# Context key/value projections as three fp16 products of split operands in place of one float32 product

## What is computed

```
# layer 0, cross-attention (context rows are layer-normed first)
k, v = split(ctx @ wkv);  q = _rope(q); k = _rope(k)
# layer 2, cross-attention
k = ctx @ Wk;  v = ctx @ Wv
# layers 1 and 3, cross-attention (W_ctx and W_k are folded to one 96 x 128 weight)
ctx = text_embed @ W_ctx + b_ctx;  k = ctx @ W_k;  v = ctx @ W_v
```

## Time and profile before

| | |
|---|---|
| time, median of 3 runs | 6562.08 us (6561.17 to 6566.58) |
| the profiled execution: its own time from first to last instruction (the span; the page gives no other) | 6568.9 us |
| TensorE busy | 6072.1 us, 92% of the span |
| VectorE busy | 4851.4 us, 74% |
| ScalarE busy | 4175.0 us, 64% |
| GpSimd busy | 2747.1 us, 42% |
| mean granted TensorE clock | 0.967 of full speed |

### The profile page before, as it was taken

How to read it: one execution, slowest core, us unless ns; L and a number is a source line. 1 busy time by engine, 2 the same in 40 slices (tenths; PEclk the granted TensorE clock), 3 DMA queues, 4 the chain that set the end, 5 groups by cost and what they waited for, 6 DMA issues and landing times.

```text
span 6568.9 us, 122562 instructions
## 1 busy us (share of the span) xinstructions
PE 6072.1 (92%) x42376; PEld 3586.6 (55%) x42376; DVE 4851.4 (74%) x9782; ACT 4175.0 (64%) x9228; POOL 2747.1 (42%) x2358
## 2 busy tenths in 40 slices
PE   7999999989899998998989999899898999989988
PEld 5566456654556645664455654566445665456644
DVE  6887776657788777675878877667578886876656
ACT  4556676656655668665765666766575566776656
POOL 3466115751246612564025651266402655126630
PEclk8999999999999999998999999999898999999989
DMA  3111011100111101111011100111001111011100
GB/s 87 36 33 26 22 35 31 28 25 19 48 34 33 27 21 37 30 32 28 13 50 36 33 27 19 38 30 33 23 18 49 31 30 30 16 41 30 28 20 12
DMA packets 347662, 204.18 MB, mean 31 GB/s; under 512 B 165005, under 2 KB 319981, under 8 KB 346926
## 3 DMA queue, kind: packets, MB, share of 16 engines
q1 hardware_dynamic: 347054, 196.34, 11.8%
HBM read 105.18 MB, written 1.05 MB: 16 GB/s over the span
## 4 chain that ended last, share of the span: by engine, by line
PE 73%; DVE 10%; ACT 7%; issue 5%; POOL 4%; SPq 1%; DVEq 0%; DMA 0%; POOLq 0%; ACTq 0%
PE ring L1347 37%; PE o_acc L1347 18%; PE scores L1347 17%; DVE max_part L2097 3%; POOL weight_sum L1309 3%; ACT probs L1782 2%; ACT qop L1636 2%; DVE o_inv L2120 1%; POOL qm L1328 1%; DVE region L2059 1%; DVE qop L2056 1%; ACT qm L1636 1%; DVE ring L2073 1%; PE ring L1451 0%; DVE ring L2076 0%
## 5 line engine op out<-in xcount | busy, mean ns | idle before, releaser
L2097 DVE TENSOR_REDUCE max_part<-ring 128x1 f32<-128x400 f32 (+2 forms) x4608 | 2412.7, 577 | 567.4 <-PE ring L1347 543.8
L1782 ACT ACTIVATE probs<-scores 128x512 f32<-128x512 f32 (+1 forms) x3840 | 2105.9, 599 | 1051.5 <-PE scores L1347 961.8
L1309 POOL TENSOR_TENSOR weight_sum<-weight_sum,probs 128x512 f32<-128x512 f32 (+1 forms) x1408 | 1785.7, 1268 | 201.9 <-ACT probs L1782 66.8
L1347 PE MATMUL o_acc<-probs,region 128*32 128x256 f32 (+2 forms) x13312 | 1348.2, 388 | 11.3 <-ACT probs L1782 6.8
L1636 ACT ACTIVATE region<-ring 64x400 f16<-64x400 f32 (+4 forms) x1744 | 820.4, 480 | 480.6 <-PE ring L1347 291.9
L1309 POOL TENSOR_TENSOR weight_sum<-probs 128x512 f32<-128x512 f32 x256 | 325.4, 1271 | 1619.5 <-PE ring L1347 1194.3
L1347 PEld LDWEIGHTS o_acc<-probs,region 128*32 128x32 f32 (+2 forms) x13312 | 586.0, 122 | 547.0 <-issue 202.4
L1347 PE MATMUL scores<-qop,region 128*128 128x256 f16 (+1 forms) x3328 | 804.1, 274 | 11.3 <-ACT qop L1636 7.8
L1347 PE MATMUL scores<-qop,x_cop 128*128 128x256 f16 (+1 forms) x3328 | 800.1, 273 | 0.0
L1347 PE MATMUL ring<-nk,qm 128*128 128x400 f16 (+2 forms) x2560 | 709.5, 337 | 51.9 <-DVE max_part L2097 19.7
L1347 PE MATMUL scores<-qm,nk 128*128 128x512 f16 (+1 forms) x1920 | 657.3, 389 | 62.1 <-ACT probs L1782 32.0
(11 more groups left out here) (170 smaller groups left out, 7265.9 us busy)
## 6 DMA issues: line engine op xcount, KB each, us to landing
x_cop<-region SPq DMA_DIRECT2D x256, 200.1 KB, 3.1
stage<-in_wide SPq DMA_DIRECT2D x512, 64.0 KB, 2.0
nk<-region SPq DMA_DIRECT2D x192, 100.1 KB, 2.2
stage<-in_wide SPq DMA_DIRECT2D x128, 128.0 KB, 2.6
v_stage<-in_wide SPq DMA_DIRECT2D x256, 64.0 KB, 1.9
wo_stage<-in_wide SPq DMA_DIRECT2D x32, 512.0 KB, 4.0
cop_few<-kop_few SPq DMA_DIRECT2D x256, 32.0 KB, 1.9
ff_w<-in_ff_w SPq DMA_DIRECT2D x24, 256.0 KB, 3.4
```

The costliest lines, as they stand in the source:

```text
L1309: pool.tensor_tensor(total, before, probs[0:rows_, (un.chunk + k) % PROBS, :], ALU.add)\
L1347: return pe.matmul(out, lhs, rhs, start=start, stop=stop, skip_group_check=True)
L1782: act.activation(to, src, ACT.Exp, scale=t.scale).then_inc(exp_done.sem, 1)
L2097: dve.tensor_reduce(dst, src, AX.X, ALU.max).then_inc(*release(one))
```

## The change

Each operand of a context projection is held as two fp16 numbers, high and low, whose sum is close to the float32 value, and the product is made as high x high + high x low + low x high in one PSUM bank. The wide weights are multiplied by 32 before they are split (`GAIN`); the scale of the exponential and that of the value copy take it out again.

- Weights of 1 and 7: once at the start, 8 groups each are read from the input blob to `region`, ScalarE writes the high half, VectorE the low half (into the space of `ctx_t` and `src_t`), and SyncE stores both to DRAM (`kv_split`). These are the 16 "split" items. A unit then loads its weights from there, in place of the float32 ones.
- Context: ScalarE writes the high half, VectorE the low half, and VectorE gives back the bank. For `src_t` ScalarE first applies scale and bias within the bank.
- The folded narrow weights get the same treatment in `fold_w`.
- The planner gets new costs, new waits and the split items, so that the lists of all engines change.

```diff
+            def in_halves(out, lhs, rhs):
+                mm(out, lhs[0], rhs[0], True, False)
+                mm(out, lhs[0], rhs[1], False, False)
+                return mm(out, lhs[1], rhs[0], False, True)
...
-                        last = mm(out[:, 0:w], stage[0:t.dk, w_at, k, W_K:W_K + P], src[0:t.dk, a0:a0 + w], True, True)
+                        if t.cross:
+                            halves = k_split_of(un)
+                            last = in_halves(out[:, 0:w], [halves[:, k, l, :] for l in range(2)],
+                                             [src[:, l, a0:a0 + w] for l in range(2)])
...
+                                last = in_halves(out[0:r, m * P:(m + 1) * P], [src[:, l, at:at + r] for l in range(2)],
+                                                 [halves[:, l, :] for l in range(2)])
...
+SPLITS = [(s, g) for s in (1, 7) for g in range(H // 2)]
...
+    for i in range(len(SPLITS)):
+        put(2.0 + 6.0 * i, "split", i)
...
+    def split(self, due, one):
+        self.part("ACT", "split", due, one, 0.4, [])
+        self.part("DVE", "split", due, one, 0.55, [("ACT", one)])
+        self.part("SP", "split", due, one, 0.6, [("DVE", one)], 4.0)
...
-            self.part("PE", "op", due, one, 0.1 + w * 0.00155, deps, 0.2)
+            self.part("PE", "op", due, one, 0.06 + w * 0.00128 if t.cross and i else 0.1 + w * 0.00155, deps, 0.2)
...
             load_hidden_weights(0)
+            sp.dma_start(kv_in[1][:, :, 0, :], a["wide1"][:, 0:DC, SK:SV].rearrange("g p c -> p g c")).then_inc(kv_loaded[0], 16)
...
+            wait((mod_full, 1))
+            for k, at in enumerate((SK, SV)):
+                sp.dma_start(kv_in[7][:, :, k, :], a["wide7"][:, 0:DC, at:at + P].rearrange("g p c -> p g c"))\
+                    .then_inc(kv_loaded[1], 16)
             program()
...
+                def split_high_weights(i):
+                    s, g = SPLITS[i]
+                    if g == 0:
+                        act.wait_ge(kv_loaded[s // 7], 48 if s == 1 else 32)
+                    copy(kv_out[s][:, g, :, 0, :], kv_in[s][:, g, :, :], scale=GAIN).then_inc(kv_high, 1)
...
                         if j < 4:
-                            last = copy(ctx_t[:, u % 2, a0:a0 + w], out[0:DC, 0:w])
+                            copy(ctx_t[:, u % 2, 0, a0:a0 + w], out[0:DC, 0:w]).then_inc(ctx_high.sem, 1)
                         else:
-                            last = copy(src_t[0:DC, u % 2, a0:a0 + w], out[0:DC, 0:w], scale=cols[0:DC, C_CLNW:C_CLNW + 1],
-                                        bias=cols[0:DC, C_CLNB:C_CLNB + 1])
+                            copy(out[0:DC, 0:w], out[0:DC, 0:w], scale=cols[0:DC, C_CLNW:C_CLNW + 1],
+                                 bias=cols[0:DC, C_CLNB:C_CLNB + 1]).then_inc(ctx_high.sem, 1)
+                            copy(src_t[:, u % 2, 0, a0:a0 + w], out[0:DC, 0:w]).then_inc(ctx_high.sem, 1)
+                        return
...
+                def context_low(one, j):
...
+                    dve.tensor_tensor(to[:, 1, :], ring[0:DC, bank(one), 0:w], to[:, 0, :], ALU.subtract).then_inc(*release(one))
```

More of the change, by code:

```diff
@@ L45, in __init__ @@
         self.chunks = self.kt * self.halves
-        self.scale = float((64 if wide else 8) ** -0.5)
+        self.gain = GAIN if cross and wide else 1.0
+        self.scale = float((64 if wide else 8) ** -0.5) / self.gain
         self.dk = DC if (cross and wide) else D
@@ L517, in job, with weights @@
         (self.wide_job if t.wide else self.narrow_job)(due, one, un, t, n, j, kind, i, k, pe)
+    def weights(self, un):
+        if un.wide_at + 2 < len(self.wide) and self.wide[un.wide_at + 2].t.cross:
+            return [("SP", ("split", len(SPLITS) - 1))]
+        return []
     def inputs(self, un):
@@ L541, in wide_job @@
             if j == t.last_op:
-                self.part("SP", "load", due, one, 2.1 if t.rope else 1.4, [pe], 2.5)
+                self.part("SP", "load", due, one, 2.1 if t.rope else 1.4, [pe, *self.weights(un)], 2.5)
         elif kind == "low":
@@ L1036, in values_of, with k_split_of, v_split_of @@
             return (x_nv if un.t.cross else nv_few)[:, un.u % 2, :, :]
+        def k_split_of(un):
+            sets = 2 if un.t.rope else 1
+            halves = stage[0:DC, un.wide_at % 2, 0:sets, :].bitcast(F16)
+            return halves[:, :, 2 * W_K:2 * W_K + 2 * P].rearrange("p s (l c) -> p s l c", l=2)
+        def v_split_of(un):
+            return v_stage[0:DC, un.wide_at % 2, :].bitcast(F16).rearrange("p (l c) -> p l c", l=2)
         def split_of(s, u, kind):
@@ L1095, in load_weights @@
                 src = blob[un.p, :, 0:sets * SQS].rearrange("p (s c) -> p s c", s=sets)
+                if un.t.cross and un.u == 0 and un.p == 0:
+                    wait((kv_stored, 16 * len(SPLITS)))
                 for k in range(sets):
@@ L1526, in wide_job @@
                         for m in range(nt):
-                            r = t.rows(t0 + m)
-                            last = mm(out[0:r, m * P:(m + 1) * P], src[0:t.dk, (t0 + m) * P:(t0 + m) * P + r],
-                                      v_stage[0:t.dk, w_at, :], True, True)
+                            r, at = t.rows(t0 + m), (t0 + m) * P
+                            if t.cross:
+                                halves = v_split_of(un)
+                                last = in_halves(out[0:r, m * P:(m + 1) * P], [src[:, l, at:at + r] for l in range(2)],
+                                                 [halves[:, l, :] for l in range(2)])
+                            else:
+                                last = mm(out[0:r, m * P:(m + 1) * P], src[:, at:at + r], v_stage[:, w_at, :], True, True)
                     elif kind == "shift":
@@ L1646, in store_values @@
                         elif m1 > m0:
-                            last = copy(to[0:n, t0 + m0:t0 + m1, :], src[0:n, m0 * P:m1 * P].rearrange("p (m c) -> p m c", c=P))
+                            last = copy(to[0:n, t0 + m0:t0 + m1, :], src[0:n, m0 * P:m1 * P].rearrange("p (m c) -> p m c", c=P),
+                                        scale=1.0 / t.gain)
                     return last
@@ L2027, in pre @@
                         load(u)
+                    elif kind == "ctx":
+                        context_low(one, j)
+                    elif kind == "fold":
+                        fold_low(one)
                     elif kind == "stats":
```

121 lines of the change are left out of this document (93 added, 28 removed).

## The result

The changed kernel takes 6530.08 us (median of 4 runs, 6529.27 to 6534.0), the kernel before 6564.33 (4 runs, 6561.17 to 6570.43): ratio 0.9949, 95% interval 0.9935 to 0.9963. It is faster by half a per cent, 34 us, where 205 were forecast; 6530 lies above the range of 6290 to 6460.

What follows compares the result with a forecast made beforehand. TensorE's own work bounds attentions 1 and 7. Of 274 us raw saving 230 arrive; less 13 for the start and 12 for context halves, 205 off 6562 gives 6357 us (own range 6310 to 6400, wider 6290 to 6460).

Steps and rivals of the forecast that it cites:

- The prices: TensorE's context projections: fp16 matmuls start 0.17 us apart at 400 columns, 0.055 at 128-column value tiles; raw sum 274 us.
- half hidden: Rival: weight loads hide only half, value matmuls 0.082 us apart, total 6484; chance 0.07.
- exposed (0.109) weight loads: Rival: each fresh 128-column fp16 load bounds its value matmul at 0.109 us, total 6616; chance 0.05.
- I take 30 of 39: Attention 1: of 39 us TensorE saves per stage, 30 arrive (ends 15 and 39), 120 us in all.
- the halves of the context: Stages of attention 0: splitting the context adds 3 us for each of four stages, 12 us (ends 0 and 30).
- the clock of 1.00 in attention 1: Attention 1: the granted clock was read as 1.00, full speed (2.4 GHz), in the kernel before.
- The rival in which VectorE takes over: Attention 1: VectorE can't be filled beyond 90%, stage ends at 404 us, 18 saved, total 6405; chance 0.17.
- Attention 7: Attention 7: no other engine is close, so 23 of 24 us per stage arrive, 92 us.
- The narrow part: Narrow attentions' context projections: 18 of 23 us saved arrive.
- The start: Program start: splitting delays the first queries to 52 us and first scores to 64, 13 us lost (ends 6 and 17).
- a load takes SyncE 0.65 us at most: Start: issue time per load on SyncE, taken as 0.5 us, so the last two loads are issued by 45.6.
- no longer late: Start: the late `v_stage` load, about 4 us of waiting before the first scores, no longer costs time.

Runs made afterwards that it cites:

- 9: Changed kernel, attention 1: TensorE's last two attn x V groups of a unit moved right ahead of the next unit's first scores; 6521.17 us, 0.9935.
- 11: Changed kernel with attention 1's last two attn x V groups moved ahead of the next first scores and its maximum over half of the columns; 6472.55 us, 0.9861.
- 7: Changed kernel's operations, but the planner reckons TensorE's context projections with the durations of the kernel before; 6496.74 us, 0.9896.
- 12: Changed kernel, VectorE computes each low half of the normed context twice, the first into a tile nothing reads; 6554.8 us, 0.9988.
- 10: Changed kernel planned with the old projection durations, and VectorE's maximum in attention 1 over half of the columns; 6447.95 us, 0.9822.
- 1: Changed kernel, ScalarE splits attention 7's weights only after TensorE has begun the first unit's values; 6531.64 us, 0.9951.
- 8: Changed kernel, weight splits later on all queues, the three loads for attention 1's splits issued behind the narrow weights; 6512.94 us, 0.992.
- 4: Changed kernel with attention 1 back in float32 (its splits, source halves and three products undone); 6537.21 us, 0.9962.

## Why the prediction was wrong

**The prices: right.** 0.17 and 0.0575 us against 0.17 and 0.055. The rivals of half hidden (0.082) and of exposed (0.109) weight loads are refuted. The Trainium skill's 81 ns a matmul (page "TensorE: Matmul & The Clock Gate", section "Back-to-back issue gap") does not hold for this stream, whose matmuls are 57 ns apart. The low half of a context piece, taken at 700 ns, lasts 684:

```profile
L2024 DVE TENSOR_TENSOR src_t<-ring,src_t 96x512 f16<-96x512 f32 x24 | 16.4, 684 | 12.5 <-ACT src_t L1725 12.5
```

**"I take 30 of 39" in attention 1: the step that failed.** It was 120 us, its low end (15 a stage) still 60; measured 2. Four things are in it.
- It weighed VectorE by its mean over the stage, 359 of 422 or 85%. That mean holds the entries and ends, where VectorE waits. In the units that repeat it was already 92.5 of 103.7, 89%, so with VectorE's work as it is the unit got from 25.9 to 24.8 at best in the orders tried (9), half of the saving; with half of the maxima it reached 24.2 (11).
- It took the order of the lists as given. The planner gets the new durations, and its new list moved ready work out of the one place where TensorE must wait for VectorE and ScalarE in turn. The new order as a whole cost 31 us in attention 1 (7), this gap about 13 of them (9). Both lists could be read beforehand, and this gap stands in the new one.
- It gave a price to the halves of the context only in the stages of attention 0, 12 us, where half of them do lie. The other half it put into VectorE's mean in attention 1 (364 of 383). If computing them once costs what computing them again did (12), those in attention 0 cost 7 and those in attention 1, which had no price, 16.
- It took the clock of 1.00 in attention 1 as given; at most 15 us went there.

These overlap and do not add up to the 118 us that are missing: the order (31) and the halves (16) make 47; halving the maxima, once the order is the old one, gave attention 1 another 37 (10). Some 34 stay unexplained.

The rival in which VectorE takes over was the nearer story, but it, too, stood on the stage's mean, and its 404 us a stage were 18 too few.

**Attention 7: right in kind, too large.** 23 of the 24 us a stage were forecast to arrive, 16.3 measured. The unit fell from 23.0 to 21.8 us, 1.2 of the 97 / 64 = 1.5 that its prices give. The rest is in the entries and the end; which of them was not tried.

**The narrow part: wrong in sign.** 18 us off forecast. Attentions 4 and 10 gave 1, and 3 and 9 lost 25. With the old reckoning these two are 10 us below the kernel before (7), so this too is the order. Which of its moves does it stays open. The longer time at half clock can account for up to 27 us, as much as the whole loss. Attention 6, not in the forecast, gave 10.5 of the 13 in the second column.

**The start: right.** Forecast 13, ends 6 and 17; measured 15. In the changed kernel:

```profile
49.08 0.94 SPq L1285 DMA_DIRECT2D region<-in_wide  x2
50.13 3.40 SPq L1186 DMA_DIRECT2D kv_split<-ctx_t  x6
...
54.26 2.56 ACT L1725 ACTIVATE src_t<-region 96x256 f16<-96x256 f32 x8 [21.70 <-DMA region<-in_wide]
56.72 1.53 ACT L1725 ACTIVATE qop<-ring 64x256 f16<-64x256 f32 x4
...
67.45 0.27 PE L1414 MATMUL scores<-qop,kop_few 128*128 128x256 f16 x1
```

The prediction's "a load takes SyncE 0.65 us at most" is wrong already in the kernel before, where the first two `narrow_w` loads take 3.69. Here the last loads are issued from 49.1 us on, not by 45.6, so the first queries come at 56.7 in place of 52 and the first scores at 67.5 in place of 64 (35.46 and 51.12 in the earlier trace rows). The prediction called the `v_stage` load "no longer late"; it is late too, and hidden behind ScalarE's wait (1, 8).

## What to carry to other kernels

When the bounding engine is to get faster, read the second engine's share in the units that repeat, not in the mean over a stage: the mean holds turns in which everybody waits, and hides how little room there is. Then follow one unit's loop of latencies (here last maximum, columns, transpose, shift copies, first scores) and see which ready work the new list leaves beside it; a planner fed with truer durations can give a worse list. Compare the granted clock stage by stage as well: new idle time in one engine went with a lower clock here. A limit that gives little when lifted alone is not refuted by that: lift the next one with it.

## What the runs showed of the hardware

SyncE's issue of the first two `narrow_w` loads took 7.34 us in the changed kernel, right behind its three new loads, and 3.69 in the kernel before. Without the three (4) it was 3.67, with the three behind the narrow weights (8) 3.64, and there the two attention 7 loads behind them took 3.13 in place of 0.94. The time of an issue, then, depended on what was issued just before it, and 3.6 us of the start's delay are of this kind.

Full fp16 loads of 128 columns, one for every matmul, hide behind matmuls 57 ns apart, with load records of 100 ns each (197 in float32). Of the three products of a tile the first two load the same high half; where the weights change the distance is the same 56 ns.

At the half clock a scores matmul starts 0.21 us after the one before it (295.40 to 295.61 us in the changed kernel), at the full clock 0.11.
